# Layer 0's projections: two buffers for the parts of q and k, and GpSimd computing the low parts

## The chip, the cores and the metric

The kernel runs on one core of a Trainium2 chip. The metric is the device time in microseconds (us) of one execution. Engines are called PE (TensorE), DVE (VectorE), ACT (ScalarE), POOL (GpSimd) and SP (SyncE, here only a queue that issues transfers); PEld is the weight load of TensorE.

## What is computed

The reference is a transformer of two layers on x of shape (2, 2048, 256). Layer 0 has a softmax attention with rotary positions, then a mixture of 16 experts; layer 1 has a linear attention, then a block that adds a second softmax attention and a mixture of 8 experts. The change touches only the first step of layer 0's attention:

```python
h = _layernorm(x, axis=-1) * (1 + ca) + sa
q = (x @ W_q.T).reshape(B, L, N_HEADS, D_HEAD)
k = (x @ W_k.T).reshape(B, L, N_HEADS, D_HEAD)
v = (x @ W_v.T).reshape(B, L, N_HEADS, D_HEAD)
rot_even = x_even * c - x_odd * s
rot_odd = x_even * s + x_odd * c
```

Here x inside the attention is h. After the rotation q and k are each split for the attention into a high part, rounded to the reduced format of TensorE (F32R), and a low part, which is what the rounding lost.

## The kernel before

The program runs as stages, each a block with its own buffers and semaphores and a barrier over all engines at its end: modulation, `project_layer0` (the one that changes), softmax attention of layer 0, experts, linear attention, projections and experts of layer 1, softmax attention of layer 1, and the last addition. The two softmax attentions take most of the time.

`project_layer0` handles 4096 tokens in 8 groups n of G = 512 tokens (two batches b, four groups q in each). For each group, engine by engine in program order:

- DVE: statistics of the next group's layer norm (L225, L229), its reciprocal and the normalized z (L236, L241); then twice, once for q and once for k, four products of the projection in PSUM with cos or sin (L369), and a difference and a sum of these (L372, L373), which are the even and odd halves of the rotated q or k, in the tile `sp_whole`. Last come the four low parts, whole minus high (L290, in `split_vector_lo`).
- ACT: the root for the next layer norm (L258); the high parts of q (L285, in `split_scalar_hi`, a = 0 and 1); the shifted, scaled and transposed h of the next group (L270); two copies of v out of PSUM (L395); the high parts of k (L285, a = 2 and 3). Every high part first waits until all stores of the group before have landed (the wait on `sp.stored`, L284), because there is one buffer of parts.
- PE: the q and k projections (L411), which wait for h of this group and for the products of the group before; the transposes of the next group's z (L251); the v projection (L418).
- SP: after the copies of v, four stores of v (L313); then for each a, after its low part, the store of the high part and that of the low part (L305), eight stores of 256 KB.
- POOL: one memset at the start (L349), then nothing.

The waits that set the order around the change: L284 (ACT's high part waits for the stores of the group before), the wait for `sp.lo_ready` ahead of L372 (DVE may not overwrite `sp_whole` before all low parts of the group before are computed), L289 (a low part waits for its high part), and L297 (a store waits for its low part).

Of the kernel before, what the change touches and what calls it, by code (L numbers as in the profile page):

```python
# [19 lines left out]
ds = bass.ds  # L20
# [296 lines left out]
def project_layer0(nc, m, io):  # L317
    with ExitStack() as ctx:
        sb, pb, sem = allocators(ctx, nc, "qkv0")
        ln, sp = ln_buffers(ctx, nc, "qkv0", ring=2), split_buffers(ctx, nc, "qkv0")  # L320
        w_qk = sb("w_qk", [P, KH, 4 * P])
        w_v = sb("w_v", [P, KH, D])
        cos, sin = sb("cos", [P, T]), sb("sin", [P, T])
        prod = sb("prod", [P, 4, G])
        va = sb("va", [P, TPG, NH * AUG])
        qk_ps = pb("qk_ps", [P, 4, G])
        v_ps = pb("v_ps", [P, TPG, D])
        loaded, ones_set = sem("loaded"), sem("ones_set")
        qk_ready, v_ready, v_copied, v_stored = sem("qk_ready"), sem("v_ready"), sem("v_copied"), sem("v_stored")
        prod_ready = sem("prod_ready")  # L330
        block = ctx.enter_context(nc.Block())

        @block.sync
        def _(sync):
            sync.dma_start(w_qk[:], io.l0_wqk).then_inc(loaded, 16)
            sync.dma_start(w_v[:], io.l0_wv).then_inc(loaded, 16)
            sync.dma_start(cos[:], io.cos).then_inc(loaded, 16)
            sync.dma_start(sin[:], io.sin).then_inc(loaded, 16)
            with sync.Fori(0, B) as b:
                with sync.Fori(0, GPB) as q:  # L340
                    n = group_of(b, q)
                    store_values(sync, io, va, v_copied, v_stored, n, b, q)
                    split_store(sync, io, sp, n, b, q, paired=True)
            sync.wait_ge(v_stored, B * GPB * 16 * NHG)
            sync.wait_ge(sp.stored, B * GPB * 16 * 4 * NPART)

        @block.gpsimd
        def _(pool):
            nc.gpsimd.memset(va[:].rearrange("p t (h c) -> p (t h) c", c=AUG)[:, :, HD:AUG], 1.0).then_inc(ones_set, 1)  # L349

        @block.vector
        def _(dve):
            dve.wait_ge(m.x_loaded[0], 16)
            ln_stats(nc, dve, m, ln, 0, 0)
            ln_normalize(nc, dve, m, ln, 0, 0, lambda: None)
            dve.wait_ge(loaded, 64)
            dve.wait_ge(m.x_loaded[1], 16)
            with dve.Fori(0, B) as b:
                with dve.Fori(0, GPB) as q:
                    n = group_of(b, q)  # L360
                    _, tile = next_group(b, q)
                    ln_stats(nc, dve, m, ln, n + 1, tile)
                    ln_normalize(nc, dve, m, ln, n + 1, tile, lambda: None)
                    c, s = cos[:, ds(q * G, G)], sin[:, ds(q * G, G)]
                    for a in range(2):
                        dve.wait_ge(qk_ready, n * 4 + 2 * a + 2)
                        dve.wait_ge(sp.whole_ready, n * 4 + 2 * a)
                        for r, (src, by) in enumerate(((0, c), (1, s), (0, s), (1, c))):
                            nc.vector.tensor_tensor(prod[:, r], qk_ps[:, 2 * a + src], by, ALU.mult).then_inc(prod_ready, 1)  # L369
                        dve.wait_ge(prod_ready, n * 8 + 4 * a + 4)  # L370
                        dve.wait_ge(sp.lo_ready, n * 4)
                        nc.vector.tensor_tensor(sp.whole[:, 2 * a], prod[:, 0], prod[:, 1], ALU.subtract).then_inc(sp.whole_ready, 1)  # L372
                        nc.vector.tensor_tensor(sp.whole[:, 2 * a + 1], prod[:, 2], prod[:, 3], ALU.add).then_inc(sp.whole_ready, 1)  # L373
                    for a in range(4):
                        split_vector_lo(nc, dve, sp, n, a)

        @block.scalar
        def _(act):
            act.wait_ge(ones_set, 1)
            ln_root(nc, act, m, ln, 0)  # L380
            ln_shift(nc, act, m, ln, 0, 0, 0, 0)
            with act.Fori(0, B) as b:
                with act.Fori(0, GPB) as q:
                    n = group_of(b, q)
                    b_next, _ = next_group(b, q)
                    ln_root(nc, act, m, ln, n + 1)
                    for a in range(2):
                        split_scalar_hi(nc, act, sp, n, a)
                    ln_shift(nc, act, m, ln, n + 1, b_next, 0, 0, lambda: act.wait_ge(v_ready, n * 2), (n + 1) % 2)
                    act.wait_ge(v_stored, n * (16 * NHG))  # L390
                    for pair in range(2):
                        act.wait_ge(v_ready, n * 2 + pair + 1)
                        dst = va[:, 2 * pair:2 * pair + 2].rearrange("p t (h c) -> p t h c", c=AUG)[:, :, :, 0:HD]
                        src = v_ps[:, 2 * pair:2 * pair + 2].rearrange("p t (h c) -> p t h c", c=HD)
                        nc.scalar.activation(dst, src, ACT.Copy).then_inc(v_copied, 1)  # L395
                    for a in range(2, 4):
                        split_scalar_hi(nc, act, sp, n, a)

        @block.tensor
        def _(pe):  # L400
            ln_tensor(nc, pe, m, ln, 0)
            pe.wait_ge(loaded, 64)
            with pe.Fori(0, B * GPB // 2) as i:
                for slot in range(2):
                    n = 2 * i + slot
                    h = ln.hT[:, slot * KH:(slot + 1) * KH]
                    pe.wait_ge(ln.h_ready, n * KH + KH)
                    pe.wait_ge(prod_ready, n * 8)
                    for a in range(4):
                        for kh in range(KH):  # L410
                            last = nc.tensor.matmul(qk_ps[:, a], w_qk[:, kh, a * P:(a + 1) * P], h[:, kh],  # L411
                                                    start=(kh == 0), stop=(kh == KH - 1))
                        last.then_inc(qk_ready, 1)
                    ln_tensor(nc, pe, m, ln, n + 1)
                    pe.wait_ge(v_copied, n * 2)
                    for t in range(TPG):
                        for kh in range(KH):
                            last = nc.tensor.matmul(v_ps[:, t], h[:, kh, t * P:(t + 1) * P], w_v[:, kh],  # L418
                                                    start=(kh == 0), stop=(kh == KH - 1))
                        if t % 2:  # L420
                            last.then_inc(v_ready, 1)
# [1454 lines left out]
```

## Time and profile before

| | |
|---|---|
| median of 3 runs | 4009.01 us |
| lowest, highest | 4007.7, 4018.12 us |
| profiled execution, its own time | 4002.33 us |
| its span in the trace | 4000.7 us |
| mean granted TensorE clock | 0.937 |
| busy over the span: PE, DVE, ACT, POOL | 89%, 84%, 64%, 4% |
| the changed stage, from its first transfer issue to the first of the next stage | 46.60 to 192.85 us |

Times in the rows are in us from the start of the span unless marked ns. In the rows of a timeline, the number in brackets is the engine's idle time just before the instruction, and the name behind the arrow is what ended it. A row of the timeline may merge several instructions of one line (x4). The tile called `sp_parts` in the code is `qkv_sp_parts` in the rows.

### The profile page before, as it was taken

How to read it: one execution, taken by the hardware profiler on the slowest of the kernel's cores; microseconds unless marked ns; L12 is line 12 of the kernel's file. 1: busy time of each engine (PE TensorE's matmuls, PEld its weight loads, DVE VectorE, ACT ScalarE, POOL GpSimd, SP SyncE). 2: the span in 40 equal slices, each digit the busy share in tenths (PEclk: the TensorE clock that was granted, in tenths of full speed). 3: DMA queues.
4: the chain of work that ended last, by engine and by line, in shares of the span. 5: the costliest groups of instructions: out<-in, count | busy, mean ns of one | idle time of the engine just before them, and what ended most of it. 6: DMA issues, size and time to landing. Idle time of an engine off the chain costs nothing. (4 is left out here: it accounts for less than half of the span.)

```text
span 4000.7 us, 89598 instructions
## 1 busy us (share of the span) xinstructions
PE 3544.1 (89%) x30184; PEld 1592.9 (40%) x30184; DVE 3366.3 (84%) x4386; ACT 2563.2 (64%) x4698; POOL 179.9 (4%) x167
## 2 busy tenths in 40 slices
PE   6679999999999998437788799879999999999997
PEld 4323333333333334414566577623333333333332
DVE  5789999998999998502566587789999998999999
ACT  1228888887888886214222222228888887888886
POOL 0000000000000000331311000000000000000000
PEclk8869999998999999769899899969999999999998
DMA  5632111201112010134100123230101201102021
GB/s 162 169 51 99 32 25 22 36 11 33 25 22 36 11 36 9 38 118 159 49 21 21 42 68 80 61 52 15 32 19 28 36 11 33 26 21 36 11 36 48
DMA packets 134450, 184.07 MB, mean 46 GB/s; under 512 B 68313, under 2 KB 87170, under 8 KB 128908
## 3 DMA queue, kind: packets, MB, share of 16 engines
q1 hardware_dynamic: 124412, 145.31, 16.3%
q0 software_dynamic: 9648, 33.63, 2.4%
q8 instruction: 236, 3.87, 0.4%
q14 instruction: 154, 1.26, 0.1%
HBM read 105.90 MB, written 73.43 MB: 45 GB/s over the span
## 5 line engine op out<-in xcount | busy, mean ns | idle before, releaser
L707 DVE TENSOR_REDUCE att_l_part_max<-att_l_max_ps 128x2 f32<-128x1024 f32 x2144 | 2598.6, 1222 | 101.3 <-PE att_l_max_ps L580 99.8
L678 ACT ACTIVATE att_l_probs<-att_l_s_ps 128x512 f32<-128x512 f32 x4096 | 2225.4, 596 | 492.5 <-PE att_l_s_ps L598 243.8
L612 PE MATMUL att_l_o_ps<-att_l_probs,att_l_v_sb 128*17 128x256 f32 x16384 | 1291.5, 387 | 25.9 <-ACT att_l_o_sb L684 16.0
L598 PE MATMUL att_l_s_ps<-att_l_q_sb,att_l_k_sb 50*128 50x512 f32 x4100 | 1033.3, 499 | 12.5 <-issue 7.7
L580 PE MATMUL att_l_max_ps<-att_l_k_sb,att_l_q_sb 50*128 50x512 f32 x4288 | 898.1, 414 | 94.0 <-DMA att_l_k_sb<-k_hi 61.0
L598 PEld LDWEIGHTS att_l_s_ps<-att_l_q_sb,att_l_k_sb 50*128 50x128 f32 x4100 | 386.5, 184 | 886.6 <-ACT att_l_probs L678 873.4
L612 PEld LDWEIGHTS att_l_o_ps<-att_l_probs,att_l_v_sb 128*17 128x17 f32 x16384 | 274.1, 95 | 769.7 <-issue 405.0
L580 PEld LDWEIGHTS att_l_max_ps<-att_l_k_sb,att_l_q_sb 50*128 50x128 f32 x4288 | 419.6, 192 | 146.2 <-DVE att_l_part_max L707 79.5
L1732 DVE SCALAR_TENSOR_TENSOR ffn_acc<-ffn_qk_ps,ffn_comb,ffn_acc 128x256 f32<-128x256 f32 x256 | 123.9, 484 | 32.7 <-PE ffn_qk_ps L1643 24.3
L1240 DVE TENSOR_TENSOR moe_hid<-moe_act_gate,moe_gf_ps 128x512 f32<-128x512 f32 x16 | 11.0, 688 | 139.4 <-PE moe_gf_ps L1189 139.4
L1217 ACT ACTIVATE moe_hT<-moe_rT_ps,all_modv 128x256 f32<-128x256 f32 x64 | 30.9, 563 | 149.4 <-PE moe_rT_ps L1180 149.4
L1180 PE MATMUL moe_rT_ps<-all_ident,moe_rows 128*128 128x128 f32 x128 | 18.3, 289 | 105.1 <-DMA moe_w_pr<-in_w_proj 105.1
L1643 PE MATMUL ffn_qk_ps<-ffn_w_hi,ffn_h_hi 128*128 128x512 f32 x256 | 102.6, 401 | 0.0
L1643 PE MATMUL ffn_qk_ps<-ffn_w_hi,ffn_h_lo 128*128 128x512 f32 x256 | 101.2, 395 | 0.0
L1643 PE MATMUL ffn_qk_ps<-ffn_w_lo,ffn_h_hi 128*128 128x512 f32 x256 | 100.9, 394 | 0.0
L1502 DVE TENSOR_TENSOR lin_masked<-lin_qk_ps,all_triu 128x1024 f32<-128x1024 f32 x64 | 75.0, 1214 | 24.9 <-PE lin_qk_ps L1339 24.9
L411 PE MATMUL qkv_qk_ps<-qkv_ln_hT,qkv_w_qk 128*128 128x512 f32 x128 | 64.1, 658 | 22.3 <-ACT qkv_ln_hT L270 18.4
L1434 ACT ACTIVATE lin_o_sb<-lin_o_ps 128x512 f32<-128x512 f32 x32 | 19.1, 597 | 98.6 <-PE lin_o_ps L1348 98.6
L1476 DVE TENSOR_SCALAR lin_qkT<-lin_qk_ps 128x512 f32<-128x512 f32 x34 | 23.4, 689 | 64.0 <-PE lin_qk_ps L1363 59.9
L1305 POOL DMA_INDIRECT lin_got<-slot_out,all_get_at x64 | 65.8, 1028 | 199.4 <-DVE all_x_res L1470 181.6
L1428 ACT ACTIVATE lin_q_one<-lin_qkT,lin_parity 128x512 f32<-128x512 f32 x32 | 20.6, 711 | 75.8 <-DVE lin_qkT L1476 75.8
L1363 PE MATMUL lin_qk_ps<-lin_ln_hT,lin_w_qk 128*128 128x512 f32 x136 | 64.8, 622 | 4.7 <-ACT lin_ln_hT L270 4.2
(214 smaller groups left out, 2357.9 us busy)
## 6 DMA issues: line engine op xcount, KB each, us to landing
att_l_k_sb<-k_hi SPq DMA_DIRECT2D x72, 256.0 KB, 8.8
att_l_q_sb<-q_hi SPq DMA_DIRECT2D x280, 64.0 KB
att_l_q_sb<-q_lo SPq DMA_DIRECT2D x140, 72.0 KB
att_l_v_sb<-v_rows SPq DMA_DIRECT2D x18, 544.0 KB, 13.6
att_l_k_sb<-k_lo SPq DMA_DIRECT2D x36, 256.0 KB, 8.8
slot_rows<-att_l_zeros POOLq DMA_DIRECT2D x8, 1024.0 KB, 13.6
moe_rows<-slot_rows SPq DMA_DIRECT2D x16, 512.0 KB
slot_out<-moe_y POOLq DMA_DIRECT2D x16, 512.0 KB
```

The costliest lines, as they stand in the source:

```text
L411: last = nc.tensor.matmul(qk_ps[:, a], w_qk[:, kh, a * P:(a + 1) * P], h[:, kh], start=(kh == 0), stop=(kh == KH - 1))
L580: last = nc.tensor.matmul(max_ps[:, r, half], q_sb[rows, j % QR, pair, tile * P:(tile + 1) * P], k_sb[rows, j // GPB % 2, pair, part * G:( ...
L598: nc.tensor.matmul(s_ps[:, (j * EXPS + u * HG + h) % SB], k_sb[rows, j // GPB % 2, pair, u * P:(u + 1) * P], q_sb[rows, j % QR, pair], sta ...
L612: last = nc.tensor.matmul(o_ps[32 * h:32 * h + AUG, cols], v_sb[:, j // GPB % 2, u, h * AUG:(h + 1) * AUG], probs[:, u % 2, h, cols], star ...
L678: nc.scalar.activation(probs[:, u % 2, h], s_ps[:, (j * EXPS + u * HG + h) % SB], ACT.Exp, scale=float(HD) ** -0.5).then_inc(exp_done, 1)
L707: nc.vector.reduce_max(part_max[:, j % 2, k], max_ps[:, r], AX.X).then_inc(slot_taken, 1)
L1217: nc.scalar.activation(hT[:, half, cols], rT_ps[:, half, cols], ACT.Identity, bias=m.modv[:, 0, 2, half, b:b + 1], scale=m.modv[:, 0, 3, h ...
L1305: nc.gpsimd.indirect_dma_start(out=got[:, t, k], out_offset=None, in_=io.slot_out, in_offset=bass.IndirectOffsetOnAxis(ap=m.get_at[:, tile ...
L1363: last = nc.tensor.matmul(qk_ps[:, a], w_qk[:, kh, a * P:(a + 1) * P], ln.hT[:, kh], start=(kh == 0), stop=(kh == KH - 1))
L1502: nc.vector.tensor_tensor(masked[:, t % 2, banks].rearrange("p r e n -> p (r e) n"), qk_ps[:, banks].rearrange("p r (e n) -> p (r e) n", n=P),
L1643: last = nc.tensor.matmul(qk_ps[:, pair], h[:, slot * KH + kh, t * P:(t + 1) * P], w[:, kh, pair * 2 * D:(pair + 1) * 2 * D], start=(kh == ...
L1732: nc.vector.scalar_tensor_tensor(acc[:, t], qk_ps[:, e // 2, (e % 2) * D:(e % 2 + 1) * D], comb[:, t, e:e + 1], acc[:, t], ALU.mult, ALU.a ...
```

## The change

Only `project_layer0` is changed.

- The buffers `whole` and `parts` exist twice, by parity of the group (`slot`). `whole` grows from 8 to 16 KB and `parts` from 16 to 32 KB in each partition. The semaphores `stored` and `lo_ready` exist once for each slot. A high part waits for the stores of the group two before, and `whole` is overwritten after the low parts of the group two before.
- The four low parts of a group are computed by POOL, in a loop of its own, with the same operation; DVE's loop ends after `whole` of k.
- The loops over b and q become one loop over four pairs of groups with the two slots written out; b and q are computed from the loop's index.
- Order and content of the stores on SP are as before; they wait for `lo_ready` of their slot.

```diff
--- before.py
+++ after.py
@@ -317,7 +317,13 @@
 def project_layer0(nc, m, io):
     with ExitStack() as ctx:
         sb, pb, sem = allocators(ctx, nc, "qkv0")
-        ln, sp = ln_buffers(ctx, nc, "qkv0", ring=2), split_buffers(ctx, nc, "qkv0")
+        ln = ln_buffers(ctx, nc, "qkv0", ring=2)
+
+        whole, parts = sb("whole", [P, 2, 4, G]), sb("parts", [P, 2, 4, NPART, G], F32R)
+        whole_ready, hi_ready, lo_ready = sem("whole_ready"), sem("hi_ready"), [sem(f"lo_ready{r}") for r in range(2)]
+        stored = [sem(f"stored{r}") for r in range(2)]
+        PAIRS_OF = B * GPB // 2
+        place = lambda i, slot: (2 * i + slot, i // (GPB // 2), i % (GPB // 2) * 2 + slot)
         w_qk = sb("w_qk", [P, KH, 4 * P])
         w_v = sb("w_v", [P, KH, D])
         cos, sin = sb("cos", [P, T]), sb("sin", [P, T])
@@ -336,17 +342,31 @@
             sync.dma_start(w_v[:], io.l0_wv).then_inc(loaded, 16)
             sync.dma_start(cos[:], io.cos).then_inc(loaded, 16)
             sync.dma_start(sin[:], io.sin).then_inc(loaded, 16)
-            with sync.Fori(0, B) as b:
-                with sync.Fori(0, GPB) as q:
-                    n = group_of(b, q)
+            with sync.Fori(0, PAIRS_OF) as i:
+                for slot in range(2):
+                    n, b, q = place(i, slot)
                     store_values(sync, io, va, v_copied, v_stored, n, b, q)
-                    split_store(sync, io, sp, n, b, q, paired=True)
+                    for a in range(4):
+                        sync.wait_ge(lo_ready[slot], i * 4 + a + 1)
+                        for part, (dram, row0) in enumerate((((io.q_hi, 0), (io.q_lo, NSHIFT)), ((io.k_hi, 0), (io.k_lo, 0)))[a // 2]):
+                            rows = dram[ds(b, 1)].rearrange("a h c t -> (a h) c t")[:, row0:row0 + HD, ds(q * G, G)]
+                            dst = rows[:, a % 2 * (HD // 2):(a % 2 + 1) * (HD // 2)]
+                            sync.dma_start(dst, parts[:, slot, a, part].bitcast(F32)).then_inc(stored[slot], 16)
             sync.wait_ge(v_stored, B * GPB * 16 * NHG)
-            sync.wait_ge(sp.stored, B * GPB * 16 * 4 * NPART)
+            for slot in range(2):
+                sync.wait_ge(stored[slot], PAIRS_OF * 16 * 4 * NPART)
 
         @block.gpsimd
         def _(pool):
             nc.gpsimd.memset(va[:].rearrange("p t (h c) -> p (t h) c", c=AUG)[:, :, HD:AUG], 1.0).then_inc(ones_set, 1)
+            pool.wait_ge(ones_set, 1)
+            with pool.Fori(0, PAIRS_OF) as i:
+                for slot in range(2):
+                    n = 2 * i + slot
+                    for a in range(4):
+                        pool.wait_ge(hi_ready, n * 4 + a + 1)
+                        nc.gpsimd.tensor_tensor(parts[:, slot, a, 1], whole[:, slot, a], parts[:, slot, a, 0].bitcast(F32),
+                                                ALU.subtract).then_inc(lo_ready[slot], 1)
 
         @block.vector
         def _(dve):
@@ -355,38 +375,41 @@
             ln_normalize(nc, dve, m, ln, 0, 0, lambda: None)
             dve.wait_ge(loaded, 64)
             dve.wait_ge(m.x_loaded[1], 16)
-            with dve.Fori(0, B) as b:
-                with dve.Fori(0, GPB) as q:
-                    n = group_of(b, q)
+            with dve.Fori(0, PAIRS_OF) as i:
+                for slot in range(2):
+                    n, b, q = place(i, slot)
                     _, tile = next_group(b, q)
                     ln_stats(nc, dve, m, ln, n + 1, tile)
                     ln_normalize(nc, dve, m, ln, n + 1, tile, lambda: None)
                     c, s = cos[:, ds(q * G, G)], sin[:, ds(q * G, G)]
                     for a in range(2):
                         dve.wait_ge(qk_ready, n * 4 + 2 * a + 2)
-                        dve.wait_ge(sp.whole_ready, n * 4 + 2 * a)
+                        dve.wait_ge(whole_ready, n * 4 + 2 * a)
                         for r, (src, by) in enumerate(((0, c), (1, s), (0, s), (1, c))):
                             nc.vector.tensor_tensor(prod[:, r], qk_ps[:, 2 * a + src], by, ALU.mult).then_inc(prod_ready, 1)
                         dve.wait_ge(prod_ready, n * 8 + 4 * a + 4)
-                        dve.wait_ge(sp.lo_ready, n * 4)
-                        nc.vector.tensor_tensor(sp.whole[:, 2 * a], prod[:, 0], prod[:, 1], ALU.subtract).then_inc(sp.whole_ready, 1)
-                        nc.vector.tensor_tensor(sp.whole[:, 2 * a + 1], prod[:, 2], prod[:, 3], ALU.add).then_inc(sp.whole_ready, 1)
-                    for a in range(4):
-                        split_vector_lo(nc, dve, sp, n, a)
+                        dve.wait_ge(lo_ready[slot], i * 4)
+                        nc.vector.tensor_tensor(whole[:, slot, 2 * a], prod[:, 0], prod[:, 1], ALU.subtract).then_inc(whole_ready, 1)
+                        nc.vector.tensor_tensor(whole[:, slot, 2 * a + 1], prod[:, 2], prod[:, 3], ALU.add).then_inc(whole_ready, 1)
 
         @block.scalar
         def _(act):
             act.wait_ge(ones_set, 1)
             ln_root(nc, act, m, ln, 0)
             ln_shift(nc, act, m, ln, 0, 0, 0, 0)
-            with act.Fori(0, B) as b:
-                with act.Fori(0, GPB) as q:
-                    n = group_of(b, q)
+            def split_hi(i, slot, a):
+                act.wait_ge(whole_ready, (2 * i + slot) * 4 + a + 1)
+                act.wait_ge(stored[slot], i * (16 * 4 * NPART))
+                nc.scalar.activation(parts[:, slot, a, 0], whole[:, slot, a], ACT.Copy).then_inc(hi_ready, 1)
+
+            with act.Fori(0, PAIRS_OF) as i:
+                for slot in range(2):
+                    n, b, q = place(i, slot)
                     b_next, _ = next_group(b, q)
                     ln_root(nc, act, m, ln, n + 1)
                     for a in range(2):
-                        split_scalar_hi(nc, act, sp, n, a)
-                    ln_shift(nc, act, m, ln, n + 1, b_next, 0, 0, lambda: act.wait_ge(v_ready, n * 2), (n + 1) % 2)
+                        split_hi(i, slot, a)
+                    ln_shift(nc, act, m, ln, n + 1, b_next, 0, 0, lambda: act.wait_ge(v_ready, n * 2), 1 - slot)
                     act.wait_ge(v_stored, n * (16 * NHG))
                     for pair in range(2):
                         act.wait_ge(v_ready, n * 2 + pair + 1)
@@ -394,7 +417,7 @@
                         src = v_ps[:, 2 * pair:2 * pair + 2].rearrange("p t (h c) -> p t h c", c=HD)
                         nc.scalar.activation(dst, src, ACT.Copy).then_inc(v_copied, 1)
                     for a in range(2, 4):
-                        split_scalar_hi(nc, act, sp, n, a)
+                        split_hi(i, slot, a)
 
         @block.tensor
         def _(pe):
```

## Rows read from the trace of the kernel before

**Rows 1.** The page's costliest groups; busy, mean ns of one, idle before them.

```profile
L707 DVE TENSOR_REDUCE att_l_part_max<-att_l_max_ps 128x2 f32<-128x1024 f32 x2144 | 2598.6, 1222 | 101.3 <-PE att_l_max_ps L580 99.8
```

**Rows 2.** Waits, 75 to 181 us: who waited for whom, total, times, longest.

```profile
ACT qkv_sp_parts L285 <- DMA k_lo<-qkv_sp_parts: 53.6, 7, 7.9
...
PE qkv_qk_ps L411 <- ACT qkv_ln_hT L270: 18.4, 6, 4.2
DVE qkv_sp_parts L290 <- ACT qkv_sp_parts L285: 8.4, 7, 1.5
```

**Rows 3.** Timeline of ACT over one group, 98 to 114 us.

```profile
98.64 1.15 ACT L285 ACTIVATE qkv_sp_parts<-qkv_sp_whole 128x512 fp32r<-128x512 f32 x2 [7.37 <-DMA k_lo<-qkv_sp_parts]
99.70 1.43 ACT L270 ACTIVATE qkv_ln_hT<-qkv_ln_zT,all_modv 128x512 f32 x2
101.02 1.08 ACT L395 ACTIVATE qkv_va<-qkv_v_ps 128x512 f32<-128x512 f32 x2
...
113.91 1.15 ACT L285 ACTIVATE qkv_sp_parts<-qkv_sp_whole 128x512 fp32r<-128x512 f32 x2 [7.66 <-DMA k_lo<-qkv_sp_parts]
```

**Rows 4.** Timeline of SP's queue, last group.

```profile
179.03 2.23 SPq L313 DMA_DIRECT2D v_rows<-qkv_va  x4
181.61 0.58 SPq L305 DMA_DIRECT2D q_hi<-qkv_sp_parts  x1
...
186.72 0.58 SPq L305 DMA_DIRECT2D k_lo<-qkv_sp_parts  x1
```

**Rows 5.** Waits of SP's queue, 40 to 260 us.

```profile
SPq L345 <- DMA k_lo<-qkv_sp_parts: 3.5, 1, 3.5
```

**Rows 6.** Busy time in stretches; then PEclk, DMA share and GB/s.

```profile
90.00:105.00 15.00, 12.87 (x45) 7.50 (x44) 13.33 (x31) 4.79 (x9) 0.00 (x0) 1.00 0.67 177
...
250.00:275.00 25.00, 19.93 (x84) 7.46 (x82) 22.17 (x23) 5.95 (x12) 0.00 (x0) 0.53 0.60 84
275.00:300.00 25.00, 25.00 (x248) 8.93 (x244) 25.00 (x26) 22.20 (x42) 0.00 (x0) 1.00 0.09 23
...
925.00:950.00 25.00, 25.00 (x176) 7.83 (x168) 16.27 (x14) 15.03 (x29) 0.00 (x0) 0.65 0.16 31
```

**Rows 7.** Timeline of DVE over one group, 103 to 119 us.

```profile
103.98 1.41 DVE L225 BATCH_NORM_STATS2 qkv_ln_stats<-all_x_res 128x6 f32 x4
...
107.80 0.68 DVE L369 TENSOR_TENSOR qkv_prod<-qkv_qk_ps,qkv_cos 128x512 f32<-128x512 f32 x1
...
110.31 0.69 DVE L372 TENSOR_TENSOR qkv_sp_whole<-qkv_prod 128x512 f32<-128x512 f32 x1
...
111.71 0.69 DVE L369 TENSOR_TENSOR qkv_prod<-qkv_qk_ps,qkv_cos 128x512 f32<-128x512 f32 x1
...
115.44 1.29 DVE L290 TENSOR_TENSOR qkv_sp_parts<-qkv_sp_whole,qkv_sp_parts 128x512 fp32r<-128x512 f32 x2
```

**Rows 8.** Timeline of PE over one group, 70 to 82 us.

```profile
70.66 7.03 PE L411 MATMUL qkv_qk_ps<-qkv_ln_hT,qkv_w_qk 128*128 128x512 f32 x16
...
78.40 3.62 PE L418 MATMUL qkv_v_ps<-qkv_w_v,qkv_ln_hT 128*128 128x256 f32 x16
```

**Rows 9.** Groups of POOL's instructions: busy, mean ns of one.

```profile
L554 POOL MEMSET att_l_k_sb<- 2x8192 f32 x4 | 27.7, 6918 | 480.1 <-POOLq L71 480.0
...
L557 POOL MEMSET att_l_zeros<- 128x2048 f32 x1 | 1.8, 1809 | 0.1
...
L349 POOL MEMSET qkv_va<- 128x64 f32 x1 | 0.2, 202 | 40.9 <-POOLq L71 40.9
```

**Rows 10.** Timeline of all engines, first group: the split.

```profile
65.74 0.69 DVE L372 TENSOR_TENSOR qkv_sp_whole<-qkv_prod 128x512 f32<-128x512 f32 x1
...
66.56 1.15 ACT L285 ACTIVATE qkv_sp_parts<-qkv_sp_whole 128x512 fp32r<-128x512 f32 x2 [6.94 <-DVE qkv_sp_whole L372]
...
69.66 0.69 DVE L372 TENSOR_TENSOR qkv_sp_whole<-qkv_prod 128x512 f32<-128x512 f32 x1
```

**Rows 11.** Timeline of DVE, last group: k's first whole.

```profile
175.47 0.69 DVE L372 TENSOR_TENSOR qkv_sp_whole<-qkv_prod 128x512 f32<-128x512 f32 x1
```

## Prediction

> **What bounds the kernel now.** Over the whole span the costly groups are those of the two softmax attentions, where DVE's row maxima [rows 1] run with PE beside them. The change touches none of that, so its worth is that of one stage of 146 us, read by itself. The page's chain of waits covers only the last microseconds of the kernel and says nothing on this stage. I read instead, in this order, the waits of the stage, the timelines of each engine over one group of 512 tokens, and the busy times.
>
> The waits name the loop. ACT's high part of q waits seven times, 53.6 us in all, for the landing of the last store of the group before, k_lo. PE waits 18.4 us for ACT's h, and DVE 8.4 us for ACT's high parts; both stand behind the same ACT wait in program order [rows 2]. The timeline of ACT gives the pitch: the high parts of two neighbouring groups start at 98.64 and 113.91, 15.3 us apart, and each start follows a wait of over 7 us [rows 3]. The loop runs so: high parts of q (1.15 us), h of the next group (1.43), copies of v (1.08), then on SP four stores of v and eight of parts, from 179.03 to 187.30 = 8.3 us in the last group [rows 4], and 3.5 us until the last one has landed [rows 5]. With the starts of ACT (1.06, 1.32 and 1.3 us to SP's first issue) the sum is 3.7 + 8.3 + 3.5 = 15.5 us, which is the pitch. No engine is full: in 15 us DVE is busy 13.3, PE 12.9, ACT 4.8, POOL 0, and the DMA engines 0.67 of the time [rows 6].
>
> **The second buffer** takes the stores out of that loop. The next limit is the longest of these, per group:
> - DVE without the low parts. Its work runs without a break from its statistics at 103.98 to its low parts at 115.44, which is 11.46 us with all its small waits [rows 7]. I take 11.5.
> - PE: q and k from 70.66, v until 78.40 + 3.62 = 82.02, so 11.4 us at the full clock [rows 8]. It must follow the products of the group before. These end some 1.4 us ahead of PE's v (the first half of q and k is there 3.6 us after PE's start, half of 7.03; DVE's products run from 107.80 to about 114.2, two `whole` of 0.6 ahead of 115.44, 6.4 us [rows 7]; 10.0 against 11.4), so PE isn't held.
> - DMA: 0.67 of 15 us is 10.0 us, in which 177 GB/s times 15 us = 2.7 MB move [rows 6]. SP's issuing: 8.3 us. ACT: 4.8 us.
> - POOL: four subtractions of 128x512, priced below.
>
> The new wait for `stored[slot]` looks two groups back. The stores of a group land about 14.1 us after its k products (2.3 until SP starts, see below, 8.3 + 3.5); the high part that needs the buffer comes two pitches after, less 69.66 - 66.56 = 3.1 us [rows 10], at 19.9 us. Slack 5.8 us, so the wait costs nothing, unless the DMA engines take half as long again. The wait for the low parts two groups back ahead of L372 is met a whole pitch early.
>
> From the first group's first `whole` of k at 69.66 [rows 10] to the last group's at 175.47 [rows 11] there are seven pitches, 105.8 us. Seven of 11.5 are 80.5: 25.3 us gained. After that, SP's first issue came 179.03 - 175.47 = 3.6 us later, since ACT's copies of v stood behind the late high parts. Now they end with PE's v, 1.4 us after the k products, plus 0.6 for the last copy and 0.3 to the issue, 2.3 us: 1.2 us more gained. The stores' issue and landing stay at the tail, as does the barrier. Gross gain 26.5 us.
>
> **The low parts on POOL.** The trace has no operation with tensor inputs on POOL. It has memsets: 202 ns for 64 elements, 1809 ns for 2048, 6918 ns for 8192 on two partitions [rows 9], that is 0.81 to 0.85 ns for each element and about 0.15 us for the instruction. One stream of 512 would be 0.15 + 0.43 = 0.58 us, the lower end. Two inputs and an output, if the three go one after the other at that rate, are 0.15 + 3 x 0.43 = 1.45 us, my upper end; DVE's own 0.65 us (1.29 for two) [rows 7] lies near the lower. I take 1.45, as it is the end that would hurt. Four are 5.8 us against a pitch of 11.5: POOL is idle half of the time, and would keep up with the pitch at up to 2.9 us each. Who waits behind it: SP's stores of k. POOL has the last low part about 5.7 us after the k products, SP comes to it at 2.3 + 6.5 = 8.8 us. So this wait is covered, and if POOL took 3 us each it would end at 8.8 and just begin to show.
>
> **DVE beside POOL.** The two never ran together on tensors here, so what POOL's reading costs DVE (or gains) is bounded only. In the first group DVE's first `whole` ran from 65.74, ACT's two high parts from 66.56 [rows 10]. POOL could start its first low part at about 67.2 and end the second at 67.2 + 2 x 1.45 = 70.1. DVE wants its `whole` of k at 69.66. If the two exclude each other, DVE loses 0.5 us in each of seven pitches, 3.5 us in all; if not, nothing. A gain is excluded, as DVE's instruction is the same. I take the middle, 1.8 us.
>
> The rule of the Trainium skill that speaks against the change stands on the page SBUF — State Buffer, Who interferes with whom: a DVE instruction with two SBUF inputs and a GpSimd instruction that reads SBUF hold a shared port exclusively, and the later one blocks. Here those are L372 and L373, not L369, which reads PSUM. By that rule the 3.5 us end holds; no row of this trace shows it. The GPSIMD Engine Reference, Performance versus the Vector engine, measured 4497 ns for 2048 fp32 with two inputs; a quarter, estimated 1.1 to 1.25 us for 512, would end the second low part by 69.7 and lose nothing even under the lock.
>
> **Sum.** 26.5 - 1.8 = 24.7 us. Against the profiled execution, 4002.3 us with a span of 4000.7, that is 3977.6. The median of the runs shown is 4009.0, 6.7 us above the profiled one; the gain taken from it gives 3984.3, my forecast. The stages behind start from a barrier and have the same work, but PE's clock may come up at another moment: the granted clock was 0.53 of full from 250 to 275 us, 1.00 from 275 to 300, and 0.65 from 925 to 950 [rows 6]. In that last stretch DVE did 16.3 us of work in 25 against 25.0 in the stretch at full clock, so one change of clock a few us earlier or later is worth a few us. I allow 5 us to either side for this; it is no direction.
>
> **Rivals.**
> - DVE and POOL take turns (the lock), with longer operations on POOL than I take. At 2.0 us each the second low part ends at 71.2, DVE loses 1.5 us in each pitch, 10.5 in all, and the gain is 16 us: 3993. At 1.6 us it is 0.7 a pitch, near the forecast. For: both ask for SBUF in the same microseconds. Against: it takes a POOL well slower than its memset rate. Chance 0.17, time 3993.
> - The gain isn't had because the transfers are the bound. DMA needs 10.0 of the new 11.5 us, a margin of 15%. If the DMA engines, fed while earlier stores are still under way, took 35% longer a group (13.5 us), the pitch would be 13.5 and the gain 105.8 - 94.5 + 1.2 - 1.8 = 10.7 us: 3998, within what can't be told from no change. For: the share is already 0.67. Against: the engines keep up with SP, as the last store lands 3.5 us after its issue [rows 5], and SP needs only 8.3 of 11.5 us. Or the gain is had and lost to the later clock; both are in this case. Chance 0.10.
> - Slower: POOL itself is the pace. From 15.3 / 4 = 3.8 us for each low part the change loses; at 5 us the pitch is 20, seven of them cost 7 x 4.7 = 33 us, and the last low parts delay the stores by (2 x 5 + 2.8) - 8.8 = 4 us more: 4046. For: no row shows such an operation of POOL. Against: it would be 3.4 times my upper end from POOL's memsets. Chance 0.04. The same operation held back by DVE's own would come to less.
>
> **How the numbers follow.** Forecast 0.69, turns 0.17, transfers or clock 0.10, POOL 0.04. A measurement of this kernel can tell about 0.3%, 12 us, from no change. The forecast and the turns are beyond it (0.86, of which I give 0.01 to the middle, as 16 us is near 12), the transfers within (0.11 with that), POOL slower, 0.04. The range: from the full gain of 26.5 us below the median with 6 us of the clock and of the runs' spread, 3976, to the transfers' case with little on top, 3999.
>
> **What would show it.** Right: no wait of ACT for a store of the parts; the high parts of q 11.5 us apart from the second group on; DVE busy over 0.95 of the stage's middle; DMA share near 0.87; the stage's end near 167 us instead of 192.85; POOL with 32 subtractions of 1.1 to 1.5 us. Turns: gaps of DVE just before L372 of k, or longer L372 and L373. Transfers: ACT waits for stores again with the DMA engines full. POOL's pace: SP waits for low parts and POOL without idle time. The prediction would be wrong if the pitch isn't below 13.5 us, or if the stage ends early and the kernel doesn't.

## The result and the profile after

The changed kernel takes 3981.97 us, median of 8 runs (3978.94 to 3988.98), against 4009.71 us of the kernel before (8 runs, 3995.21 to 4027.1): a ratio of 0.9933 with a 95% interval of 0.9916 to 0.9951, or 27.7 us less. The forecast was 3984.3 us, 24.7 us less.

The profiled execution took 3984.76 us with a span of 3983.1. The changed stage ends, by the next stage's first transfer, at 164.86 us instead of 192.85: 28.0 us earlier. The waits of the changed kernel from 75 to 150 us, read as in [rows 2]:

```profile
POOL qkv_parts L368 <- ACT qkv_parts L403: 43.9, 13, 5.2
ACT qkv_parts L403 <- DVE qkv_whole L392: 35.0, 8, 5.6
...
PEld qkv_qk_ps L434 <- DVE qkv_prod L389: 2.6, 6, 0.5
```

ACT's high parts wait for no store any more. They wait for DVE's `whole`. PE waits 2.6 us in six groups for DVE's products, and the profile has no wait of DVE for PE there: DVE now sets the pitch. The same in busy time, over four pitches, with the columns of [rows 6]:

```profile
103.00:149.00 46.00, 45.84 (x161) 27.32 (x161) 42.90 (x101) 20.76 (x37) 20.07 (x17) 1.00 0.91 230
```

DVE is busy 42.9 of 46 us, 0.93, with only small waits of its own chain between. POOL is busy 20.1 us, and the DMA share is 0.91 instead of 0.67. DVE over one group, as in [rows 7], from k's first `whole` of one group to that of the next:

```profile
104.46 0.69 DVE L392 TENSOR_TENSOR qkv_whole<-qkv_prod 128x512 f32<-128x512 f32 x1
...
105.67 1.40 DVE L225 BATCH_NORM_STATS2 qkv_ln_stats<-all_x_res 128x6 f32 x4
...
108.18 1.38 DVE L241 TENSOR_SCALAR qkv_ln_z<-all_x_res,qkv_ln_mv,qkv_ln_rstd 128x256 f32 x4
...
116.00 0.69 DVE L392 TENSOR_TENSOR qkv_whole<-qkv_prod 128x512 f32<-128x512 f32 x1
```

116.00 - 104.46 = 11.54 us. The seven pitches are 12.26, 11.55, 11.45, 11.54, 11.44, 11.54 and 11.45, in all 81.2 us from 69.20 to 150.43, where [rows 10, 11] have 105.8. POOL beside it:

```profile
101.97 2.52 POOL L368 TENSOR_TENSOR qkv_parts<-qkv_whole,qkv_parts 128x512 fp32r<-128x512 f32 x2 [5.03 <-ACT qkv_parts L403]
105.89 2.49 POOL L368 TENSOR_TENSOR qkv_parts<-qkv_whole,qkv_parts 128x512 fp32r<-128x512 f32 x2 [1.40 <-ACT qkv_parts L403]
```

A low part on POOL takes 1.27 us, two take 2.51, about twice the 1.29 of DVE [rows 7]. POOL's pair for q starts when ACT's first high part is there and ends at 104.49, and DVE's first `whole` of k begins at 104.46. POOL's pair for k ends at 108.38, and DVE's normalization begins at 108.18. Neither DVE instruction is longer than before the change (0.69, and 1.38 for four), so an overlap of up to 0.2 us in the records cost nothing. The experiments show what a little more costs.

### The profile page after: what moved, and what is told of

Its sections match the earlier page's. It is cut to its first block and busy times, and to the rows that moved or that the text cites. A ratio compares the mean times of both kernels' runs of the same rounds, so it can differ in the third digit from the quotient of the medians.

```text
span 3983.1 us, 89540 instructions
## 1 busy us (share of the span) xinstructions
PE 3546.8 (89%) x30184; PEld 1593.1 (40%) x30184; DVE 3346.7 (84%) x4354; ACT 2566.2 (64%) x4698; POOL 221.3 (6%) x199
## 3 DMA queue, kind: packets, MB, share of 16 engines
q14 instruction: 153, 1.25, 0.1%
## 5 line engine op out<-in xcount | busy, mean ns | idle before, releaser
L945 POOL DMA_INDIRECT slot_rows<-z_all,post_put_at x64 | 64.2, 1003 | 104.8 <-DVE all_get_at L1129 85.6
```

What stands on the lines that cost most here:

```text
L945: nc.gpsimd.indirect_dma_start(out=io.slot_rows, out_offset=bass.IndirectOffsetOnAxis(ap=put_at[:, b, k, t:t + 1], axis=0), in_=m.z_all[:, ...
```

## The experiments

Each is compared by its stage in one profile: the mean pitch of k's first `whole` (the first of the seven left out, as it is not like the others: 14.01 us before, and 12.26 in the changed kernel, where it holds a collision of DVE with POOL), and the time of the next stage's first transfer. Before: 15.30 us and 192.85. Changed: 11.50 us and 164.86. The stage begins between 46.2 and 47.6 us in all of them, and the first group's first `whole` of k starts between 69.2 and 71.3. That spread of up to 2 us stands before the work that was changed, and it is contained in every end of a stage. The pitch is steadier: the variant with a shorter tail, whose groups are those of the changed kernel, has 11.50 again. The three variants on the buffers, on POOL alone and on the tail were run 6 to 10 times. The other five were run once, and only their profile is read.

**The buffers alone.** In the changed kernel POOL's loop goes, and DVE's loop ends with the four low parts:

```diff
+                    for a in range(4):
+                        dve.wait_ge(hi_ready, n * 4 + a + 1)
+                        nc.vector.tensor_tensor(parts[:, slot, a, 1], whole[:, slot, a], parts[:, slot, a, 0].bitcast(F32),
+                                                ALU.subtract).then_inc(lo_ready[slot], 1)
...
```

> The two buffers alone, the low parts still on DVE. My theory (the stores leave the loop, then the longest engine sets the pitch): DVE needs 11.5 + 4 x 0.65 = 14.1 us a group, with little waits 14.2, so the pitch goes from 15.1 (mean of seven) only to 14.2, 6.4 us, and with an earlier tail of 1 to 3 us the next stage's first transfer is issued near 184 to 185 us instead of 192.85: 8 us of the 28 that the whole change gives. Rival (the buffer is all of it, DVE has room): pitch near 11.6 and the stage's end near 165 us.

Measured: pitch 13.91 us, next stage at 181.71, and for the whole kernel a ratio of 0.9972 (0.9957 to 0.9987), 4005.7 us against 4014.5 of the kernel before, run beside it. DVE's timeline has no gap left:

```profile
112.20 0.69 DVE L384 TENSOR_TENSOR qkv_whole<-qkv_prod 128x512 f32<-128x512 f32 x1
...
113.41 2.49 DVE L388 TENSOR_TENSOR qkv_parts<-qkv_whole,qkv_parts 128x512 fp32r<-128x512 f32 x4
115.81 1.40 DVE L225 BATCH_NORM_STATS2 qkv_ln_stats<-all_x_res 128x6 f32 x4
```

The buffers give 11.1 of the 28.0 us, three more than my theory had. Its pitch was 14.2, but the rest of a group is 11.5 and the four low parts, which run without waits now, are 2.40 from the first start to the next statistics (115.81 - 113.41), 13.9 in all. That is 2 us over seven pitches. The tail, from k's last first `whole` to the next stage, is 13.9 us instead of 17.4, a gain of 3.5 where I had expected 1 to 3. Against that, the first group's first `whole` of k started 0.9 us later than before.

**POOL alone.** In the kernel before, DVE's calls of `split_vector_lo` go, and POOL gets a loop:

```diff
+            with pool.Fori(0, B * GPB) as n:
+                for a in range(4):
+                    pool.wait_ge(sp.hi_ready, n * 4 + a + 1)
+                    nc.gpsimd.tensor_tensor(sp.parts[:, a, 1], sp.whole[:, a], sp.parts[:, a, 0].bitcast(F32),
+                                            ALU.subtract).then_inc(sp.lo_ready, 1)
...
```

> The low parts on POOL alone, with one buffer as before. My theory: ACT's high parts still wait for the stores of the group before, the loop of ACT, SP and landing is as it was, pitch 15.3, the stage's end between 191 and 194 us, no gain. Rival (taking work from DVE is worth something by itself): a pitch of 14 or less and an end near 184 us.

Measured: pitch 15.59 us, next stage at 194.44, ratio 1.0005 (0.9990 to 1.0021). With the first pitch, which is 12.35 us here, the seven sum to 105.9 us, as before (105.8), and the 1.6 us are lost in the tail. ACT's wait for the stores is longer:

```profile
ACT qkv_sp_parts L285 <- DMA k_lo<-qkv_sp_parts: 76.0, 7, 11.2
```

It is 76.0 us instead of 53.6 [rows 2], so the time that DVE gave up went into waiting. DVE met POOL here too (its normalization takes 633 ns in the mean instead of 408), and over the seven pitches that cost nothing, as DVE isn't the pace. Neither half gives the 28 us, and they don't add up to it either: 11.1 and -1.6. The buffers make DVE the pace, and only then is it worth something to unload DVE.

**More work on POOL, twice.** One more subtraction ahead of each low part:

```diff
                     for a in range(4):
                         pool.wait_ge(hi_ready, n * 4 + a + 1)
+                        pool.wait_ge(spare_set, n * 4 + a + 1)
+                        nc.gpsimd.tensor_tensor(spare[:, 0], whole[:, slot, a], parts[:, slot, a, 0].bitcast(F32), ALU.subtract).then_inc(spare_set, 1)
...
```

> The changed kernel with one more subtraction of the same operands on POOL ahead of each low part, written to a spare tile: 2.5 us for each low part, 10.2 us a group, still below the pitch of 11.6. If POOL and DVE only meet in time (no lock): pitch 11.6, stage's end 165 to 166 us. If an instruction of POOL that reads SBUF and DVE's L392 and L393 exclude each other: each whole of k waits up to the end of a POOL instruction, pitch 12.5 to 13, stage's end 171 to 175 us, and DVE's idle time or long durations stand at L392 or the one-input instructions that reach for the second port (one normalization took 1225 ns instead of 408 beside POOL in the changed kernel).

Measured: pitch 15.44 us, next stage at 192.06. All but 0.8 us of what the change gives is gone, though POOL works only 8 x 1.39 = 11.1 us of each 15.4. From DVE's timeline and then POOL's:

```profile
115.77 1.78 DVE L396 TENSOR_TENSOR qkv_whole<-qkv_prod 128x512 f32<-128x512 f32 x1
117.47 1.75 DVE L397 TENSOR_TENSOR qkv_whole<-qkv_prod 128x512 f32<-128x512 f32 x1
...
121.66 3.22 DVE L241 TENSOR_SCALAR qkv_ln_z<-all_x_res,qkv_ln_mv,qkv_ln_rstd 128x256 f32 x4
```

```profile
115.73 1.27 POOL L371 TENSOR_TENSOR qkv_spare<-qkv_whole,qkv_parts 128x512 f32<-128x512 f32 x1
116.95 1.73 POOL L372 TENSOR_TENSOR qkv_parts<-qkv_whole,qkv_parts 128x512 fp32r<-128x512 f32 x1
118.64 1.72 POOL L371 TENSOR_TENSOR qkv_spare<-qkv_whole,qkv_parts 128x512 f32<-128x512 f32 x1
...
121.55 1.26 POOL L371 TENSOR_TENSOR qkv_spare<-qkv_whole,qkv_parts 128x512 f32<-128x512 f32 x1
```

The two `whole` of k take 1.78 and 1.75 us instead of 0.69, and POOL's subtractions between them 1.73 and 1.72 instead of 1.27: the engines take turns. In every other group only the second of the two is held, for 1.76 us. The four normalizations take 3.22 us instead of 1.38. The groups of the whole stage add up to the loss:

```profile
L241 DVE TENSOR_SCALAR qkv_ln_z<-all_x_res,qkv_ln_mv,qkv_ln_rstd 128x256 f32 x32 | 27.7, 926 | 0.6 <-DVE qkv_ln_rstd L236 0.3
...
L397 DVE TENSOR_TENSOR qkv_whole<-qkv_prod 128x512 f32<-128x512 f32 x16 | 19.5, 1220 | 0.0
L396 DVE TENSOR_TENSOR qkv_whole<-qkv_prod 128x512 f32<-128x512 f32 x16 | 15.5, 967 | 0.9
```

Against 408, 684 and 692 ns, a group loses 4 x 0.52 + 2 x 0.54 + 2 x 0.28 = 3.7 us of the 3.9 by which its pitch is longer. So the exclusion is real, and larger than I had expected (12.5 to 13), because the normalization, an instruction with one tensor input, is held up too, and loses most in all (2.1 of the 3.7 us).

**The same time on POOL, writing only.**

```diff
...
                                                 ALU.subtract).then_inc(lo_ready[slot], 1)
+                        nc.gpsimd.memset(spare[:], 0.0).then_inc(spare_set, 1)
...
```

> The changed kernel with a memset of 1312 elements (about 1.25 us by the rows of POOL's memsets) on POOL behind each low part: POOL is as busy as in the run with two subtractions, but the added half only writes. If the exclusion is between DVE's second input and POOL's reading: no delay from the added half, pitch 11.6 to 11.8, stage's end 165 to 167 us. If any instruction of POOL blocks DVE: as in the run with two subtractions, 171 to 175 us.

Measured: pitch 15.21 us, next stage at 190.43. The expectation that an added half which only writes costs nothing failed, but not for every instruction. DVE's groups over the stage, then the second `whole` of one k, then POOL beside it:

```profile
L241 DVE TENSOR_SCALAR qkv_ln_z<-all_x_res,qkv_ln_mv,qkv_ln_rstd 128x256 f32 x32 | 29.5, 983 | 0.6 <-DVE qkv_ln_rstd L236 0.3
...
L397 DVE TENSOR_TENSOR qkv_whole<-qkv_prod 128x512 f32<-128x512 f32 x16 | 19.5, 1222 | 0.0
...
L396 DVE TENSOR_TENSOR qkv_whole<-qkv_prod 128x512 f32<-128x512 f32 x16 | 11.1, 692 | 0.9
```

```profile
115.74 1.76 DVE L397 TENSOR_TENSOR qkv_whole<-qkv_prod 128x512 f32<-128x512 f32 x1
```

```profile
115.20 1.75 POOL L371 TENSOR_TENSOR qkv_parts<-qkv_whole,qkv_parts 128x512 fp32r<-128x512 f32 x1
116.90 1.19 POOL L373 MEMSET qkv_spare<- 128x1312 f32 x1
```

The `whole` waited for the subtraction, which ended at 116.95, and ran until 117.50, beside a memset that had started at 116.90. The memset took 1.19 us, as all 32 do in the mean. In the run before, the instruction in its place, a subtraction, was stretched from 1.27 to 1.72 us. So a memset and an instruction with two SBUF inputs run side by side, and for `whole` the expectation held. The first `whole` (L396) kept its 692 ns.

The normalization is another matter. Two instructions of one group of four, and POOL beside them:

```profile
119.93 0.84 DVE L241 TENSOR_SCALAR qkv_ln_z<-all_x_res,qkv_ln_mv,qkv_ln_rstd 128x256 f32 x1
...
120.69 2.62 DVE L241 TENSOR_SCALAR qkv_ln_z<-all_x_res,qkv_ln_mv,qkv_ln_rstd 128x256 f32 x1
```

```profile
119.44 1.19 POOL L373 MEMSET qkv_spare<- 128x1312 f32 x1
120.77 1.26 POOL L371 TENSOR_TENSOR qkv_parts<-qkv_whole,qkv_parts 128x512 fp32r<-128x512 f32 x1
121.97 1.19 POOL L373 MEMSET qkv_spare<- 128x1312 f32 x1
```

The first started under a memset, met no subtraction, and took 0.84 us instead of 0.41, until 120.77, just behind the memset's end at 120.63. The other took 2.62 us, until 123.31: past POOL's subtraction (to 122.03) and past its memset (to 123.16). So a memset, which reads nothing, does hold up this DVE instruction. 4 x (983 - 408) + 2 x (1222 - 684) ns = 3.4 of the 3.7 us by which the pitch is longer.

The page SBUF — State Buffer, Who interferes with whom, of the Trainium skill names both cases: two SBUF inputs against POOL's reads and not against its writes alone, and two-port modes of one-input instructions against anything on POOL. The first agrees with the 1.73 to 1.78 us beside a subtraction and the 1.19 us of the memset beside `whole`. For the second the mode is only inferred, and this case doesn't confirm it: the normalizations start 0.35 us apart for 256 columns, DVE's products 0.60 for 512, which shows no doubled rate, yet the normalization is blocked as that rule says.

**POOL later by 0.43 us.** A subtraction of 128 columns, 0.46 us, ahead of each pair:

```diff
                         pool.wait_ge(hi_ready, n * 4 + a + 1)
+                        if a % 2 == 0:
+                            pool.wait_ge(spare_set, n * 2 + a // 2 + 1)
+                            nc.gpsimd.tensor_tensor(spare[:], whole[:, slot, a, 0:128], parts[:, slot, a, 0, 0:128].bitcast(F32),
+                                                    ALU.subtract).then_inc(spare_set, 1)
...
```

> The changed kernel with a subtraction of 128 columns (0.3 to 0.5 us) on POOL ahead of each pair of low parts; POOL stays busy under 6.5 of 11.6 us. In the changed kernel POOL's pair for q ends at 104.49 and DVE's first whole of k starts at 104.46; the pair for k ends at 108.38 and the normalization starts at 108.18. If the change escapes the exclusion only by that timing: both are missed now, whole of k waits 0.3 to 0.5 us, the normalization loses 0.3 us or more (and the next low part waits in turn), pitch 12.0 to 13, stage's end 168 to 175 us. If there is slack: pitch 11.6, end 165 us.

Measured: pitch 12.40 us, next stage at 171.50, 6.6 us later than in the changed kernel. Of these 1.1 us stand ahead of the first `whole` of k and are spread; from there on 5.6 us are lost.

```profile
107.82 1.07 DVE L398 TENSOR_TENSOR qkv_whole<-qkv_prod 128x512 f32<-128x512 f32 x1
...
111.93 1.82 DVE L241 TENSOR_SCALAR qkv_ln_z<-all_x_res,qkv_ln_mv,qkv_ln_rstd 128x256 f32 x4
```

```profile
105.85 2.50 POOL L374 TENSOR_TENSOR qkv_parts<-qkv_whole,qkv_parts 128x512 fp32r<-128x512 f32 x2
...
110.14 2.48 POOL L374 TENSOR_TENSOR qkv_parts<-qkv_whole,qkv_parts 128x512 fp32r<-128x512 f32 x2
```

The first `whole` of k takes 1.07 (0.69) while POOL's pair for q ends at 108.35, and the normalizations 1.82 (1.38) while the pair for k ends at 112.62. Over the stage:

```profile
L398 DVE TENSOR_TENSOR qkv_whole<-qkv_prod 128x512 f32<-128x512 f32 x16 | 14.8, 927 | 0.9
L241 DVE TENSOR_SCALAR qkv_ln_z<-all_x_res,qkv_ln_mv,qkv_ln_rstd 128x256 f32 x32 | 14.4, 510 | 0.6 <-DVE qkv_ln_rstd L236 0.3
```

2 x (927 - 692) + 4 x (510 - 408) ns = 0.88 of the 0.90 us by which the pitch is longer. So the pitch follows DVE's own time, as it must where DVE sets it. POOL is busy 6 of 12.4 us. The changed kernel escapes these collisions by its timing alone, and 0.43 us is more than its slack.

**POOL three times.** As the second run on POOL, with two subtractions to spare tiles ahead of each low part.

> The changed kernel with two more subtractions on POOL for each low part, 3.8 us each and 15.3 a group without waiting: the rival of the prediction in which POOL itself is the pace, and at its break-even of 3.8 us. By the prediction's price (no exclusion) the pitch is 15.3 and the stage ends near 192 us. With the exclusion seen with two subtractions (POOL 1.39 us in the mean): 4 x 3 x 1.35 to 1.4 = 16.2 to 16.8 us a group, stage's end 197 to 203 us, slower than before the change.

Measured: pitch 17.37 us, next stage at 209.43, later than both ends I gave, and 16.6 us later than before the change.

```profile
75.00:175.00 100.00, 74.85 (x233) 41.95 (x232) 95.90 (x141) 29.31 (x52) 91.11 (x70) 0.93 0.65 155
```

POOL is busy 91.1 of 100 us, DVE 95.9, and both hold the time in which they are held up by the other: neither alone fills the pitch, they wait for one another in turn.

**Four more stores a group.** The high parts once more, to a spare tensor in DRAM:

```diff
                             sync.dma_start(dst, parts[:, slot, a, part].bitcast(F32)).then_inc(stored[slot], 16)
+                            if part == 0:
+                                sync.dma_start(io.again[ds(n, 1), a].rearrange("n p t -> (n p) t"), parts[:, slot, a, part].bitcast(F32)).then_inc(stored[slot], 16)
...
```

> The changed kernel with the four high parts of each group stored once more, to a spare tensor: 1.05 MB and four issues of 0.65 us more a group. The DMA engines were busy 0.91 of 11.5 us = 10.5 us, of which the 2.05 MB of parts at 380 GB/s or so are 5.4; so 10.5 + 2.7 = 13.2 us now. If DMA becomes the bound there: pitch 13.2, ACT waits for stores again, stage's end 176 to 180 us. If the slack is larger than the share says: pitch 11.6, end 167 to 169 us for the longer tail.

Measured: next stage at 176.63, which is in the range that I gave for the DMA bound, but not by the way I gave, a pitch of 13.2. The seven pitches are 12.25, 11.56, 11.45 and 11.54, as in the changed kernel, and then 11.95, 12.71 and 12.28.

```profile
ACT qkv_parts L405 <- DMA k_lo<-qkv_parts: 12.6, 2, 6.5
...
ACT qkv_va L420 <- DMA v_rows<-qkv_va: 3.4, 4, 1.2
```

The surplus costs nothing for some groups; then ACT waits for stores again (12.6 us in two groups) and for the stores of v (3.4 us), and the tail from k's last first `whole` to the next stage is 21.6 us instead of 14.4. Of the 11.8 us by which the stage ends later, 2.1 stand ahead of the first `whole` of k, before any of these stores, 2.5 are in the seven pitches and 7.2 in the tail: with 8 groups most of the backlog is paid at the end. The 2.5 are DVE meeting POOL again: its first `whole` takes 780 ns in the mean against 692, 16 times, and its normalization 476 against 434, 32 times, 2.8 us more in all. ACT's waits shift POOL's work, which is the likely reason. How far the changed kernel stands from this bound can't be read from its DMA share:

```profile
75.00:165.00 90.00, 77.30 (x274) 46.34 (x272) 76.83 (x166) 35.07 (x62) 36.14 (x29) 0.97 1.08 293
```

The share is 1.08 here, at 293 GB/s, where the changed kernel has 0.91 at 230. So 0.91 was not the end of what the transfers could do.

**A shorter tail.** The last pair of groups stands behind SP's loop, and the last group's stores of v are issued by ACT behind its own loop:

```diff
+                    if not (last and slot == 1):
+                        store_values(sync, io, va, v_copied, v_stored, n, b, q)
...
+            with sync.Fori(0, PAIRS_OF - 1) as i:
+                store_pair(i)
+            store_pair(PAIRS_OF - 1, last=True)
...
+            n, b, q = place(PAIRS_OF - 1, 1)
+            store_values(act, io, va, v_copied, v_stored, n, b, q)
```

> An attempt to beat both: the changed kernel with the four stores of v of the last group issued by ACT after its last high part, so that SP can issue that group's stores of q as soon as their low parts are there. Pitch as in the changed kernel. The last store is issued 3 to 3.5 us earlier (bounded by POOL's last low part), the stage ends near 161.5 us instead of 164.9. Whole kernel: 3 to 3.5 us less than the changed one, which its spread from run to run hides; against the kernel before 0.992 to 0.993. If the landing and not the issue bounds the tail, less than 1 us is gained.

Measured: 3979.57 us, median of 6 runs, ratio to the kernel before 0.9929 (0.9913 to 0.9946); next stage at 165.03 with k's last first `whole` at 151.39, a tail of 13.6 instead of 14.4 us. SP's last two issues:

```profile
155.66 1.79 SPq L355 DMA_DIRECT2D k_hi<-qkv_parts  x1
157.49 1.53 SPq L355 DMA_DIRECT2D k_lo<-qkv_parts  x1
```

SP starts q's stores 1.2 us ahead of k's last first `whole` instead of 3.4 us behind it, but its last two issues now take 1.79 and 1.53 us instead of 0.55 and 0.58, and it waits 4.6 us for the landing (3.9 in the changed kernel). What holds the issues isn't shown; transfers ahead of them that are still under way would do it. So the landing bounds the tail more than the issue does, and 0.8 us is gained instead of the 3 to 3.5 that I hoped for. This kernel's median can't be told from that of the changed one (3981.97 us).

## Why the prediction was right, and where not

The step that carried it, that the stores' landing closes the loop of ACT and SP and that a second buffer takes it out, is shown by the run with the buffers alone and by the run with POOL alone. The sum was 25.3 + 1.2 - 1.8 = 24.7 us, and the stage gained 24.6 + 2.95 + 0.46 = 28.0: the terms, against the profile after:

- **Seven pitches.** 25.3 us predicted, less 1.8 for DVE beside POOL, together 23.5. Measured are 105.8 - 81.2 = 24.6 with all that POOL costs. DVE's 11.5 us a group holds to 0.1; the missing 0.7 is the first pitch, 12.26, and that is the collision told below, not a second loss.
- **What paces.** I had DVE 11.5 and PE 11.4 and took the v projection to end 1.4 us after the k products. DVE starts its products 5.0 us after PE's start (139.00 and 144.00 in the last group), not 3.6, as its normalization comes first, so it trails, and PE's v ends at 150.47, with k's first `whole` at 150.43. This mis-sized the tail: predicted 1.2 us of gain, measured 17.38 - 14.43 = 2.95.

```profile
151.35 2.14 SPq L313 DMA_DIRECT2D v_rows<-qkv_va  x4
...
158.77 0.58 SPq L354 DMA_DIRECT2D k_lo<-qkv_parts  x1
164.86 0.83 SPq L521 DMA_DIRECT2D att_l_q_sb<-q_hi  x2
```

SP's first issue for the last group comes 0.9 us after that `whole` instead of 3.6 [rows 4, 11], 2.6 us of the 2.95. The k products of the first group, and with them the whole chain, are 0.46 us earlier than before [rows 10] in a stage that began 0.85 later; PE's first projections took 8.63 us instead of 9.54. The change doesn't touch them, and in the other runs this start lies up to 1.6 us later than before, so the 0.46 is spread between runs and no gain; 27.5 us are the change's.
- **A low part on POOL.** I took 1.45 us, the upper end from POOL's memsets; it is 1.27. The estimate of 1.1 to 1.25 from the Trainium skill's GPSIMD Engine Reference, Performance versus the Vector engine, was nearer.
- **DVE beside POOL.** I took 1.8 us between 0 and 3.5. In the changed kernel the exclusion cost 0.8: in the third group's normalization, within the first pitch, where one instruction took 1225 ns instead of 408.

```profile
L241 DVE TENSOR_SCALAR qkv_ln_z<-all_x_res,qkv_ln_mv,qkv_ln_rstd x36: 401/408/1225, 51.5 to 143.7; 128x256 f32 x32, 128x256 f32<-128x256 f32 x4
```

The place was wrong, though: I had only L372 and L373 in the price, and left the normalization out. The runs with POOL twice and POOL late show it is held up as much as they are. That the forecast came so near is in part luck: at the 1.45 us that I took, POOL's pair for q would end 0.36 us later than it did, and 0.43 us later cost 5.6 us in the run with POOL late. My estimate from these two is a loss of some 4.7 us at my own price, above the upper end of 3.5; the shorter subtraction spared it.
- **The rival of turns** was right in its mechanism and too cheap. I had a gain of 16 us left at 2.0 us for each low part. At 2.5 us, given as two subtractions, it was 0.8 us (192.06), and 0.43 us of delay alone cost 5.6 us.
- **The slower rival** had its turning point at 3.8 us for each low part. With the exclusion it is at 2.5 us, where the stage ends at 192.06 against 192.85. At 3.8 us the stage is 16.6 us slower, not equal. The turning point was nearer than I had it.
- **Transfers.** DMA share 0.91, near the 0.87 I wrote. No wait for a store came back; four more stores a group brought it back.
- **The signs.** Met: the waits, the pitch of 11.5, and POOL's 32 subtractions. The stage ended at 164.86, not near 167, by the shorter tail and the single collision. DVE is busy 0.93 of the middle and not over 0.95, as its waits on its own chain and on ACT's root stayed.
- **The clock behind the stage.** In the two profiles the part after the stage is 10.4 us longer in the changed kernel (3983.1 - 164.86 = 3818.2 against 3807.8), in which nothing was changed. PE's granted clock is most of the difference. The stretch from 575 us after the stage's end, before and after:

```profile
767.85:792.85 25.00, 24.01 (x238) 8.59 (x240) 23.57 (x25) 21.00 (x40) 0.00 (x0) 1.00 0.04 10
```

```profile
739.86:764.86 25.00, 22.87 (x184) 7.59 (x184) 19.01 (x21) 16.59 (x32) 0.00 (x0) 0.80 0.10 24
```

Clock 1.00 against 0.80, and DVE's row maxima fell back with PE, 19.0 busy us instead of 23.6. Summed over the 3800 us behind the stage in pieces of 25 us, each times one less its clock, the time lost is 224 us before and 232 after. The difference of 8 us covers most of the 10. Of the eight variants above seven have 231 to 235 us and a rest of 3818 to 3825 us, so it is the profiled execution before that was short, and not the changed kernel that is slow behind the stage. Its own time, 4002.33 us, also lies 7.4 below its median. The variant with more stores has 248 us and a rest of 3838; why is open. The medians, 27.7 us apart, agree with the stage's 28.0.

## What to carry to other kernels

When a loop closes over a store's landing, a second buffer is worth the difference to the next longest engine, so unload that engine in the same step; each half alone gave 11 and -2 of 28 us here. Work moved to POOL must be placed in time as well as in sum: look at which DVE instructions run in the same microseconds and leave room there, since POOL at 11 of 15 us took back all but 0.8 us of the gain, and at half load, 0.43 us later than it was, a fifth of it. And compare a change of one stage by that stage's end in the trace, because the unchanged part differed by 10 us between two profiles, with PE's granted clock.

## What the runs showed of the hardware

- A POOL subtraction with two SBUF inputs (128x512, 1.27 us alone) and a DVE instruction with two SBUF inputs (0.69 us alone) take turns: where they met in full, in the run with POOL twice, they took 1.72 to 1.75 and 1.75 to 1.80 us.
- A POOL memset doesn't take part in this: it ran beside the second half of DVE's `whole` in the run with memsets, and took 1.19 us there as elsewhere.
- A DVE tensor_scalar from SBUF with two scalars for each partition (128x256, 0.41 us alone) is held up by POOL's subtraction and by its memset: 0.84 us beside a memset alone, 2.62 us beside a subtraction and the memset behind it. DVE's statistics (407 to 414 ns) and its products from PSUM (678 to 684 ns) kept their durations in all runs.
- The issue of a 256 KB store by SP took 0.55 us, and up to 1.79 us at the end of the run with the shorter tail.
- The DMA share of the profile went above 1: 1.08 at 293 GB/s in the run with four more stores a group.
